# GpSimd takes VectorE's small work of the second dispatch, and the last two expert tiles stay on chip

## The reference

```python
x = x + attention(_layernorm(x), ctx_1024, W_q, W_kv, W_out, ln_gamma, ln_beta)   # 16 heads of 64
...
logits = xn @ Wg + bg                                   # xn = _layernorm(x)
probs = softmax(logits)
top_v, top_i = top_k(probs, 2)
top_v = top_v / (top_v.sum(-1, keepdims=True) + 1e-06)
combine = einsum('bsk,bske->bse', top_v, one_hot(top_i, 8))
for e in range(8):
    h = silu(xn @ W1[e] + b1[e]) * (xn @ W3[e] + b3[e])   # 128 -> 512
    out = out + combine[..., e:e+1] * (h @ W2[e] + b2[e]) # 512 -> 128
x = x + out
```

## Time and profile before

| what | before |
|---|---|
| median of 3 runs | 163.03 us (162.93 to 163.41) |
| the profiled execution | 163.78 us |
| its span, from first to last instruction | 161.7 us |
| TensorE busy | 136.9 us, 85% of the span |
| VectorE busy | 103.7 us, 64% |
| ScalarE busy | 76.2 us, 47% |
| GpSimd busy | 75.3 us, 47% |
| share of the chain that ended last | TensorE 66%, VectorE 13%, DMA 7%, ScalarE 7%, issue 3% |

### The profile page before, as it was taken

One profiled execution on the slowest core, in us unless ns is written; L12 is line 12 of the kernel. 1 busy time (PEld: TensorE's weight loads), 2 busy tenths in 40 slices (PEclk: granted clock), 3 DMA queues, 4 the chain that ended last, 5 costly groups with the idle time before them and its releaser, 6 DMA issues.

```text
span 161.7 us, 3923 instructions
## 1 busy us (share of the span) xinstructions
PE 136.9 (85%) x1152; PEld 128.4 (79%) x1152; DVE 103.7 (64%) x324; ACT 76.2 (47%) x210; POOL 75.3 (47%) x93
## 2 busy tenths in 40 slices
PE   6788896999999999897899899999999999993000
PEld 6677785779998999886778799999999999992000
DVE  0536699989899967988769744535363544444084
ACT  3078356857464698700633335363544545363000
POOL 3630002946553685104810777777777763334000
PEclk9999999999999999999999999999999999999755
DMA  4899910020000001338751399888868868001553
GB/s 136 268 329 285 231 33 0 0 114 19 2 2 4 0 0 46 102 99 287 230 152 70 88 323 307 267 243 247 254 195 247 272 212 276 32 27 41 153 140 97
DMA packets 21597, 23.57 MB, mean 146 GB/s; under 512 B 2333, under 2 KB 14457, under 8 KB 21577
## 3 DMA queue, kind: packets, MB, share of 16 engines
q1 hardware_dynamic: 19968, 20.30, 41.9%
q0 software_dynamic: 1440, 2.95, 6.3%
q10 hardware_dynamic: 169, 0.08, 0.2%
HBM read 19.91 MB, written 3.41 MB: 144 GB/s over the span
## 4 chain that ended last, share of the span: by engine, by line
PE 66%; DVE 13%; DMA 7%; ACT 7%; issue 3%; POOL 1%; SPq 1%; ACTq 0%; POOLq 0%; DVEq 0%
PE psum L1261 26%; PE psum L1274 12%; PE psum L1308 8%; PE psum L1290 5%; DMA early<-in_L_xattn_W_kv_dram 4%; PE psum L1037 2%; PE psum L1039 2%; PE psum L1038 2%; DMA y_back<-y_scratch 2%; DVE prob L753 2%; DVE xn L1030 2%; DVE negmax L748 2%; PE psum L1248 2%; ACT g_room L569 2%; DVE x L1027 1%
## 5 line engine op out<-in xcount | busy, mean ns | idle before, releaser
L1261 PE MATMUL psum<-probT,w 128*128 128x128 f32 x368 | 45.5, 276 | 1.7 <-issue 1.1
L987 DVE SCALAR_TENSOR_TENSOR probT<-psum,bias_col,prob 128x128 f32<-128x128 f32 x92 | 26.0, 343 | 29.7 <-ACT prob L667 29.0
L1261 PEld LDWEIGHTS psum<-probT,w 128*128 128x128 f32 x368 | 43.0, 192 | 2.5 <-issue 2.0
L667 ACT ACTIVATE prob<-psum,bias_col 128x128 f32<-128x128 f32 x92 | 26.2, 368 | 36.0 <-PE psum L1261 36.0
L513 POOL DMA_INDIRECT g_room<-xf_scratch,idx x22 | 22.0, 1000 | 22.1 <-DVE idx L963 8.8
L488 POOL TENSOR_TENSOR prob<-prob,rowsum 128x1232 f32<-128x1232 f32 x8 | 18.0, 2249 | 22.6 <-DVE rowsum L744 22.6
L1274 PE MATMUL psum<-w,probT 128*128 x184 | 25.0, 279 | 0.1
L522 POOL DMA_INDIRECT y_scratch<-xnT,out_row x18 | 17.6, 979 | 13.6 <-DVE xnT L996 10.6
L1274 PEld LDWEIGHTS psum<-w,probT 128*128 128x128 f32 x184 | 22.6, 191 | 0.8 <-issue 0.6
L1308 PE MATMUL psum<-vo,probT 128*128 128x128 f32 (+1 forms) x160 | 19.3, 276 | 0.0
L1308 PEld LDWEIGHTS psum<-vo,probT 128*128 128x128 f32 (+1 forms) x160 | 18.5, 192 | 0.0
(11 more groups left out here) (166 smaller groups left out, 180.2 us busy)
## 6 DMA issues: line engine op xcount, KB each, us to landing
w<-in_L_ffn_W_dram SPq DMA_DIRECT2D x54, 256.0 KB, 3.8
early<-in_L_xattn_W_kv_dram SPq DMA_DIRECT2D x2, 512.0 KB, 7.2
y_back<-y_scratch SPq DMA_DIRECT2D x4, 256.0 KB, 3.7
x_sb<-in_x_dram SPq DMA_DIRECT2D x2, 256.0 KB, 5.3
early<-in_L_xattn_W_q_dram SPq DMA_DIRECT2D x1, 512.0 KB, 7.0
early<-in_L_xattn_W_out_dram SPq DMA_DIRECT2D x1, 512.0 KB, 9.5
early<-in_L_ffn_b_dram SPq DMA_DIRECT2D x1, 512.0 KB, 4.8
xf_scratch<-xf SPq DMA_DIRECT2D x2, 256.0 KB, 2.6
```

The lines of the kernel that those rows point to most:

```text
L667: act.activation(silu[:, j % 2, c, :], psum[:, 2 * (j % 2), c * P:(c + 1) * P], ACT.Silu, bias=bias_col[:, 0, bass.ds(expert, 1), c]).then ...
L987: dve.scalar_tensor_tensor(out=hT[:, j % 2, c, :], in0=psum[:, 2 * (j % 2) + 1, c * P:(c + 1) * P], scalar=bias_col[:, 1, bass.ds(expert[j ...
L1261: ins = pe.matmul(psum[:, 2 * (j % 2) + a, c * P:(c + 1) * P], w13[:, j % WR, a, c * P:(c + 1) * P], xt[:, j % XR, :], start=True, stop=True)
```

## The change

Five edits that belong together:

1. `taken_blocks`, the expert numbers of the second dispatch (`other_experts`) and the one-hot `perm` of the last two token tiles move from VectorE to GpSimd, where they are written as more and smaller instructions, most with a semaphore wait between them (sums along a row are made by halving).
2. VectorE loads the expert register of tile 0 ahead of writing the first indices, and those of tiles 1 to 4 together behind tile 0's products, ahead of `other_tiles`. TensorE loads its own behind the first half of a tile's `up`. The logits of the last two token tiles go ahead of tile 0's `up`.
3. The gates are ready early: GpSimd subtracts the largest logit, ScalarE's Exp of the first six token tiles goes ahead of the Silu table, and the powers of the last two tiles are made on GpSimd. The gates are transposed on TensorE and stored by SP to a small table in DRAM.
4. Tiles 21 and 22 are not scattered. GpSimd gathers their rows' gates, VectorE makes for each tile a one-hot of slot against all 1024 tokens with the gate as its value (`back_to`), and TensorE adds `back_to` x y into two banks that hold the result of all eight token tiles. It adds the residual x2 to the same banks with the identity, and, for the second half of the tokens, the rows loaded back with diagonals of the gates that GpSimd has made. Since slots of tiles 21 and 22 are never written to `y_scratch`, two stores fill it with zeros early on.
5. The loads of `y_scratch` wait for scatters 0 to 20. SP issues those of the first half and ScalarE those of the second. The first half is summed by ScalarE and VectorE, the second by TensorE; each half is one store.

```diff
+            sp.dma_start(gate_dram[PAD_ROW:PAD_ROW + P, :], zero_rows[:, 0:1]).then_inc(gate_st, 16)
+            for k in range(K):
+                row = k * (N + P)
+                sp.dma_start(y_dram[row:row + N, :].rearrange("(t p) d -> p t d", p=P),
+                             zero_rows[:, :].rearrange("p (o d) -> p o d", o=1).broadcast_to([P, T, P])).then_inc(y_zero, 16)
...
+                elif j == 2 * FULL + 4:
+                    sp.wait_ge(gateT_ok, 1)
+                    for k in range(K):
+                        row = k * (N + P)
+                        sp.dma_start(gate_dram[row:row + N, :].rearrange("(t p) o -> t (p o)", p=P),
+                                     gateT[k * T:(k + 1) * T, :]).then_inc(gate_st, 16)
                 expert_weights(j)
...
+            def last_powers():
+                shift_logits(groups[2], G, shift_2_ok)
+                pool.wait_ge(base_e_ok, 1)
+                pool.wait_ge(shift_2_ok, 1)
+                pool.tensor_tensor(expo[:, FIRST:T, :].rearrange("p t e -> p (t e)"), base_e[:, :],
+                                   shifted[:, FIRST:T, :].rearrange("p t e -> p (t e)"), ALU.pow).then_inc(expo_2_ok, 1)
...
             AHEAD = 8
+            taken_blocks()
             for j in range(1, AHEAD):
                 if j == 2:
                     rstd_step(TWICE + G - 1)
+                elif j == 3:
+                    gone_blocks()
+                elif j == FULL:
+                    last_perm()
+                    other_experts()
                 gather(j)
-            for j in range(NT):
+            last_powers()
+
+            def gather_gates():
+
+                pool.wait_ge(gate_st, 16 * (1 + K))
+                for n in range(DIRECT):
+                    j = NT - DIRECT + n
+                    pool.indirect_dma_start(slot_gate[:, n:n + 1], None, gate_dram[:, :],
+                                            bass.IndirectOffsetOnAxis(ap=idx[:, j:j + 1], axis=0)).then_inc(slot_gate_ok[n], 16)
+
+            def gate_diagonals():
+
+                pool.wait_ge(gate_ok, 1)
+                for t in range(TB):
+                    for k in range(K):
+                        ins = pool.tensor_scalar(diag[:, t, k, :], ident[:, :], gate_w[:, k, TB + t:TB + t + 1], None, ALU.mult)
+                ins.then_inc(diag_ok, 1)
+
+            pool.wait_ge(y_zero, 16 * K)
+            for j in range(NT - DIRECT):
                 if j + AHEAD < NT:
                     gather(j + AHEAD)
                 scatter(j)
+                if j == NT - AHEAD:
+                    gather_gates()
+                    gate_diagonals()
...
-            act.wait_ge(shift_ok, 1)
-            act.activation(expo[:, :, :], shifted[:, :, :], ACT.Exp).then_inc(expo_ok, 1)
+            for n in range(YR):
+                act.wait_ge(y_st[n], 16 * len(range(n, NT - DIRECT, YR)))
+            for k in range(K):
+                row = k * (N + P) + BANK
+                act.dma_start(y_back[:, k, TB:T, :],
+                              y_dram[row:row + BANK, :].rearrange("(t p) d -> p t d", p=P)).then_inc(back[1][k], 16)
+            act.wait_ge(gate_ok, 1)
+            act.wait_ge(back[0][0], 16)
+            for t in range(TB):
+                act.activation(y_back[:, 0, t, :], y_back[:, 0, t, :], ACT.Copy, scale=gate_w[:, 0, t:t + 1]).then_inc(first_w, 1)
+            act.wait_ge(own_mm, 2)
+            act.activation(xn[:, TB:T, :], OWN_AT[1].rearrange("p (t d) -> p t d", d=P), ACT.Copy).then_inc(o_ok_2, 1)
+            act.wait_ge(o_ok_2, 1)
+            act.dma_start(out_rows[:, TB:T, :], xn[:, TB:T, :]).then_inc(stored, 16)
...
+            expert = {}
+
+            def load_expert(j):
+
+                if j == FULL:
+                    dve.wait_ge(eid_ok, 1)
+                expert[j] = dve.value_load(eid[0:1, j:j + 1], min_val=0, max_val=E - 1)
+
+            dve.wait_ge(eid_1_ok, 1)
+            load_expert(0)
...
             gated(0)
+            for j in range(1, FULL):
+                load_expert(j)
             other_tiles()
-            one_hots(2)
             gated(1)
             other_rows()
-            other_experts()
             bias_down(0)
             for j in range(2, NT + 1):
                 if j < NT:
                     gated(j)
                 bias_down(j - 1)
-                if j == FULL:
-                    dve.tensor_tensor(shifted[:, :, :], top_v[:, :, :], top_v[:, :, 0:1].broadcast_to([P, T, E]),
-                                      ALU.subtract).then_inc(shift_ok, 1)
-
-            gates()
-            for t in range(T):
-                if t % TB == 0:
-                    dve.wait_ge(back[t // TB], 16 * K)
-                dve.scalar_tensor_tensor(out=x2[:, t, :], in0=y_back[:, 0, t, :], scalar=gate_w[:, t, 0:1], in1=x2[:, t, :],
-                                         op0=ALU.mult, op1=ALU.add).then_inc(half_sum, 1)
-                dve.wait_ge(half_sum, t + 1)
-                dve.scalar_tensor_tensor(out=xn[:, t, :], in0=y_back[:, 1, t, :], scalar=gate_w[:, t, 1:2], in1=x2[:, t, :],
-                                         op0=ALU.mult, op1=ALU.add).then_inc(o_ok, 1)
+                if j == 2:
+                    other_out_rows()
+                elif j == 3:
+                    direct_tokens()
+                elif j == FULL + 3:
+                    gates()
+                elif j == FULL + 6:
+                    dve.wait_ge(gateT_mm, 1)
+                    dve.tensor_copy(gateT[:, :], GATE_AT).then_inc(gateT_ok, 1)
+                elif NT - AFTER <= j < NT - AFTER + DIRECT:
+                    back_to_tokens(j - NT + AFTER)
+
+            dve.wait_ge(back[0][1], 16)
+            for t in range(TB):
+                dve.wait_ge(first_w, t + 1)
+                dve.scalar_tensor_tensor(out=xn[:, t, :], in0=y_back[:, 1, t, :], scalar=gate_w[:, 1, t:t + 1], in1=y_back[:, 0, t, :],
+                                         op0=ALU.mult, op1=ALU.add).then_inc(second_s, 1)
+            dve.wait_ge(second_s, TB)
+            dve.wait_ge(own_mm, 1)
+            dve.tensor_tensor(xn[:, 0:TB, :], xn[:, 0:TB, :], OWN_AT[0].rearrange("p (t d) -> p t d", d=P), ALU.add).then_inc(o_ok, 1)
...
+            def own_rows(n):
+
+                j = NT - DIRECT + n
+                pe.wait_ge(back_to_ok, n + 1)
+                pe.wait_ge(y_ok, j + 1)
+                for t in range(T):
+                    ins = pe.matmul(own_at(t), back_to[:, n, t * P:(t + 1) * P], y_sb[:, j % YR, :], start=False,
+                                    stop=(n == DIRECT - 1 and t == TB - 1), skip_group_check=True)
+                    if n == DIRECT - 1 and t == TB - 1:
+                        ins.then_inc(own_mm, 1)
...
+            pe.wait_ge(gateT_ok, 1)
+            pe.wait_ge(xt_ok, NT)
+            for t in range(T):
+                pe.matmul(own_at(t), ident[:, :], x2[:, t, :], start=(t % TB == 0), stop=False, skip_group_check=True)
+            for n in range(DIRECT):
+                own_rows(n)
+            pe.wait_ge(diag_ok, 1)
+            for k in range(K):
+                pe.wait_ge(back[1][k], 16)
+                for t in range(TB, T):
+                    ins = pe.matmul(own_at(t), diag[:, t - TB, k, :], y_back[:, k, t, :], start=False,
+                                    stop=(k == K - 1 and t == T - 1), skip_group_check=True)
+            ins.then_inc(own_mm, 1)
```

More of the change, by code:

```diff
@@ L13 @@
+import math
 from contextlib import ExitStack
@@ L266, in build @@
         shift_ok = sem("shift_ok")
+        shift_2_ok = sem("shift_2_ok")
+        base_e_ok = sem("base_e_ok")
         expo_ok = sem("expo_ok")
-        back = [sem(f"back{n}") for n in range(B)]
-        half_sum = sem("half_sum")
+        expo_2_ok = sem("expo_2_ok")
+        iota_n_ok = sem("iota_n_ok")
+        y_zero = sem("y_zero")
+        gate_ok = sem("gate_ok")
+        gateT_mm = sem("gateT_mm")
+        gateT_ok = sem("gateT_ok")
+        gate_st = sem("gate_st")
+        slot_gate_ok = [sem(f"slot_gate_ok{n}") for n in range(DIRECT)]
+        back_to_ok = sem("back_to_ok")
+        diag_ok = sem("diag_ok")
+        own_mm = sem("own_mm")
+        back = [[sem(f"back{n}{k}") for k in range(K)] for n in range(B)]
+        first_w = sem("first_w")
+        second_s = sem("second_s")
         o_ok = sem("o_ok")
+        o_ok_2 = sem("o_ok_2")
         stored = sem("stored")
@@ L523, in scatter, with over_pairs, step @@
                                         y_sb[:, j % YR, :], None).then_inc(y_st[j % YR], 16)
+            def over_pairs(ap, n):
+                return ap.rearrange("p (o e) -> p o e", o=1).broadcast_to([P, n, E])
+            first_floors = floor_i[:, 0:FIRST, :].rearrange("p t k -> p (t k)")
+            first_masks = mask[:, 0:FIRST, :, :].rearrange("p t k e -> p (t k) e")
+            steps = [0]
+            def step(ins):
+                ins.then_inc(p_taken, 1)
+                steps[0] += 1
+                pool.wait_ge(p_taken, steps[0])
```

(16 more changed lines are left out.)

172 lines of the change are left out of this document (120 added, 52 removed).

## The result

The change made the kernel slower, by half a percent: 164.48 us median of 20 runs (163.69 to 168.42) against 163.56 for the kernel before on the same chip, a ratio of 1.0055 [1.0031, 1.0078]. I had forecast 160.7. (Medians, here and in the table of runs, are over all executions, while the ratios and their intervals leave out those that were longer at a lower granted clock, so the two can differ, most in run 1, where that is five of ten and the median of the others is 161.41.)

What follows compares the result with a forecast made beforehand. Bound: a full TensorE from 95.78, then a 14.9 us relay of scatter, loads, sums and store. With GpSimd's slack used up and a shorter tail, the span fell 2.4 from 161.7 to 159.3; forecast 160.7 us, range 159.0 to 162.6.

Steps and rivals of the forecast that it cites:

- eight diagonals: GpSimd between scatters 15 and 16: gate diagonals at 0.28 us each, between rows of 0.24 and 0.62.
- all slack is gone by scatter 16: GpSimd's 6.7 us of slack used up: scatter 16 at 141.5, scatter 20 at 146.6, 2.6 us later.
- The second dispatch: VectorE's other_tiles starts at 85.5, 1.7 us late; gather 5 at 89.85, 1.25 late.
- The loads: VectorE's four register loads in a row ahead of other_tiles: 1.2 to 2.4 us, taken as 2.4.
- the first indices' delay: Tile 0's register load, taken as 0.8 us, between keys and indices on VectorE: indices 0.45 later, at 74.25.
- The stall at tile 14: TensorE waits for weights queued on SP behind the gates' copy: 0.6 us (0 to 1.3).
- TensorE's 155.3: End of TensorE's work with 64 extra passes at 0.112, 7.2 us, if its clock holds.
- The power: GpSimd's power of 16 columns after gather 7: 2.96 us, 3.35 with a subtraction.
- y_back all there: Loads of y_back, issued from 148.95 on two queues behind scatter 20, all landed at 154.4.
- A: Rival: GpSimd work is cheap and register loads overlap, TensorE alone sets the end: 159.3 us; chance 0.2.
- B: Rival: GpSimd's steps and VectorE's key chain hold each other up, 164.2 us; chance 0.1 full, 0.12 part.
- C: Rival: tail is latency, loads hinder each other or TensorE's clock falls: 162.4 to 163.0 us; chance 0.1.

Runs made afterwards that it cites:

- run 1: Changed kernel with only the eight gate diagonals moved from GpSimd to ScalarE, two each behind tiles 11 to 14: 163.51 us, ratio 0.9874 to the kernel before.
- Run 6: Changed kernel with the gate diagonals still on GpSimd, each multiplied by the gate, then by 1.0, in one instruction: 163.09 us, ratio 0.9957 to before.
- run 5: Changed kernel with only VectorE's register loads back in their old places, the small dispatch work staying on GpSimd: 163.04 us, ratio 0.9961 to before.
- Run 12: Changed kernel with diagonals on ScalarE, gate stores two tiles later and register loads back; small dispatch work stays on GpSimd: 159.66 us, ratio 0.9757 to before.
- run 2: Changed kernel with only the two gate stores moved two tiles later on SP: 164.72 us, ratio 1.0088 to the kernel before.
- run 3: Changed kernel with gate diagonals on ScalarE and gate stores two tiles later on SP: 161.00 us, ratio 0.9828 to the kernel before.
- run 9: Changed kernel with the residual added by VectorE instead of TensorE, VectorE also emptying the second half: 165.10 us, ratio 1.0101 to before.
- run 7: Changed kernel with diagonals on ScalarE, gate stores two tiles later, small dispatch work and register loads back on VectorE: 159.72 us, ratio 0.9773 to before.

## Why the prediction was wrong

**The step that failed: "eight diagonals, between 0.24 (two columns) and 0.62 (512), 0.28 each".** The path was right, GpSimd's up to the last scatter with TensorE close behind; the size of this term was not. The diagonals took 0.59 at the median, 1.03 beside VectorE's large one-hot, 5.11 in all (with their issue) against 2.24. The two rows between which I interpolated are different forms: the 0.24 is one operation on two columns, the 0.62 two operations on 512. Run 6 shows that the form matters, 0.38 against 0.59 for the same 128 columns, so the line drawn through both was no line of either. The trace of before had a hint: the same step on four columns, in two operations, took less than the 0.24 of two columns in one.

```profile
5.33 0.20 POOL L466 TENSOR_SCALAR rstd<-mv 128x4 f32<-128x4 f32 x1 [3.27 <-DVE mv L707]
```

The 0.59 lies inside the bounds that I had stated, close to the upper one. With 0.62 each, the sum would have been 8 x (0.62 - 0.28) = 2.7 higher, 163.4: no gain, and outside my range. Nothing covered the error: I had written that all slack is gone by scatter 16, so 2.87 us went through; the table shows 2.81 of it between scatters 15 and 16. Runs 1 and 6 bear this out from two sides.

**The second dispatch was late by 0.55 more.** The loads cost about what I said: 0.43 of the first indices' delay against 0.45, and the second dispatch began 2.0 late against 1.7. (The 0.45 was luck: a load of 0.8 from 73.25 ends at 74.05, which is +0.25, and I named nothing for the rest.) The first indices came 0.39 later still, by instructions beside GpSimd's steps (below), and behind the indices gather 5 followed 0.54 later where it was 0.27 before, since GpSimd had just written the experts' numbers. Without the loads, runs 5 and 12 have gather 5 earlier by 1.46 and 1.19.

**TensorE.** The stall at tile 14 was 1.75 (0.6, bound 1.3): SP's stores waited for the gates as foreseen, and the weights landed in 5.1 at the median instead of 3.8. A pass cost 0.112 as taken, and the diagonals ended with the loads as I said; but the sum reads as if TensorE's 155.3 mattered by itself. In the changed kernel it does not: TensorE waits 0.49 for the last load, and coming 2 us earlier gained nothing (run 2). It stands right behind: with scatter 16 earlier by 5.0 or 2.3 (runs 1 and 6) the chain runs through TensorE, and the end moves by 1.4 and 1.65.

**Right steps.** The power 2.95 (2.96), the spacing 1.28, y_back all there 5.5 us behind its first issue (5.45), TensorE and the loads ending together. The last store and its wait took 3.4 where I had up to 3.1. By the table the misses are 0.60 to scatter 15, 2.81 to scatter 16, 0.11 to scatter 20, 0.19 to the last pass and 0.24 behind it: 3.95.

**The rivals.** *A* (cheap GpSimd) fell with the power row. *B* (steps that hold each other up) gave the right sign, not by its mechanism. A hold is there, in rows: `hit` 0.45 against 0.22, the next instruction 0.28 against 0.17, a GpSimd step of 0.55 beside VectorE's 0.71 us `perm`; the first indices pay 0.39. The Trainium skill (SBUF — State Buffer, "Who interferes with whom") says that a VectorE instruction with two SBUF inputs and a GpSimd one that reads SBUF keep each other out; these rows agree, but most such pairs in the stretch show no delay, and the `hit` of runs 3, 5 and 9, with the same steps on GpSimd, fell clear of it with 0.22. Run 12 against run 7 puts the whole price at nothing that can be measured. The slower side that I had missed was mis-sizing on a saturated engine. *C* (clock) did not happen in the profiled execution of the changed kernel, 1.00 to the end, but it did in run 2.

The chance of 0.82 for faster was too high for this reason: three unknown GpSimd prices added up on an engine whose slack the sum itself had used up. Power and loads I took at or near the upper ends of their ranges, the diagonals near the lower end, and no rival carried their upper one.

## What to carry to other kernels

Add up what is put on an engine against its slack, in the stretch in front of its last hand-over: GpSimd had 6.7 us ahead of scatter 20 and was given 10.8 (power and subtraction 3.2, gate gathers and diagonals 7.6). Price an instruction from a row of its own form; where no such row exists, carry the upper bound through the sum and see whether the verdict holds. And where two engines end together, an edit on the one behind can show nothing by itself (run 2), and one on the other less than it takes off (run 1: 5.0 us off scatter 16, 1.4 off the end), so try the pair.

## What was not expected of the hardware

- GpSimd's tensor_scalar that multiplies by a column is slower alone than followed by a multiplication by 1.0: 0.59 against 0.38 us for 128x128 in float32.
- In these rows its time, in the form of one operation, goes by columns and not by partitions: 144 columns on one partition took 0.66, near the 0.59 of 128 columns on 128, and 512 columns (float16) took 1.51. The two instructions shown are comparisons, not multiplications like the diagonals:

```profile
83.45 1.51 POOL L634 TENSOR_SCALAR perm<-perm 128x512 f16<-128x512 f16 x1
...
87.02 0.66 POOL L647 TENSOR_SCALAR ended<-ended 1x144 f32<-1x144 f32 x1
```

- A wait of 2.44 us at the end of TensorE's program was followed by a granted clock of 0.57 (run 2), and one of 2.24 at tile 14 by passes at 0.50 (run 9), while one of 0.49 left it at 1.00 (the changed kernel).
